# Routing weights of layer 1's experts: four products and on-chip transfers in place of sixteen products

## The chip, the cores and the metric

The kernel runs on one core of a Trainium2 chip. The metric is the device time of one execution in microseconds (us); a lower time is better. Three runs of the kernel before took 902.49, 902.59 and 903.48 us, so the median is 902.59 us.

## The reference, cut to what matters

The program is an eight-layer stack over x of shape (8, 256, 128), that is 2,048 tokens of 128 features, with a context of (8, 64, 128). Attention and feed-forward layers alternate. The change touches one of them, the mixture of experts of layer 1:

```
logits = x @ gate_w.T;  scores = sigmoid(logits)            # 64 experts
... the best 4 of 8 groups, then the best 8 experts of a token
topk_w = topk_w / (sum(topk_w) + 1e-20) * 2.5
rw = zeros((T, 64)).at[token, topk_idx].add(topk_w)         # (2048, 64) routing weights
expert_out[e] = (silu(x @ Wg[e].T) * (x @ Wu[e].T)) @ Wd[e].T    # hidden width 88
routed = einsum('eth,te->th', expert_out, rw)
shared = (silu(x @ Sg.T) * (x @ Su.T)) @ Sd.T               # hidden width 176
x = x + routed + shared
```

Every expert is computed for every token; the routing weight scales the expert's hidden values before the product with Wd.

## The kernel before, in words

Tokens lie on the free axis, as four groups q of 512 columns; weights, hidden units and features lie on the 128 partitions. The 64 experts' 88 hidden units are dealt into 44 chunks of 128 rows, so that 11 chunks in a row belong to the same 16 experts' share, eight rows for each expert: row p of a chunk has a routing weight of expert 16 e + p // 8, where e is the chunk's number modulo 4. A unit n is one chunk with one token group: 176 units, written out for the first 16 (`chunk_group1(0, True)` on TensorE, s = 0 to 15), then in a loop of 16 units a turn.

For each unit TensorE makes a gate product into bank s % 2 and an up product into bank 2 + s % 2 (`gate_up1`), three matmuls each, since an fp32 operand is split in a high and a low half of type fp32r and the two halves of both sides are multiplied in three of four pairs. ScalarE applies Silu to the gate (`silu1`). VectorE multiplies up by silu and then by the routing row (`hidden1`, lines 1852 and 1857; `hid_done`). ScalarE rounds the result to its high half (`hidden1_high`, line 925; `hh_hi`), GpSimd subtracts to get the low half (`hidden1_low`, line 734; `hh_lo`), and TensorE makes the down product of unit n three units behind (`down1`), into banks 4 to 7, which gather over all chunks. Weights come by DMA from SyncE's queue, and are halved by ScalarE (`gate_up1_high`, `down1_high`) and GpSimd (`gate_up1_low`, `down1_low`), one chunk ahead.

Nothing orders the work but the order in which each engine's program is written and its semaphore waits. Each engine runs its instructions in order.

Before the down products can start, the routing weights have to be spread. `rwb` is a tile of 128 partitions by 4 quarters e by 2,048 tokens: rwb[p, e, t] is the weight of expert 16 e + p // 8 for token t. The kernel before makes it so, in `routing_rows` and its counterparts:
- VectorE ends the routing with four multiplications (line 1834, `rw_done`); GpSimd copies each result beside itself (line 746, `rw_twice`), so that a transposed row is there twice.
- TensorE transposes 16 blocks (line 2501) into banks 4 to 7, after the copy of all four shared-expert results out of those banks (`sd_sb`). ScalarE copies each bank, rounded, into `rwr` (`rwr_hi`), and VectorE subtracts, for the lower 64 rows, the rounded value from the exact one (line 1842, `rwr_lo`): rows 0 to 63 of rwr are the high halves, rows 64 to 127 the low ones.
- TensorE multiplies `selr`, a 0/1 matrix that picks and repeats rows, with rwr: 16 products of 128x512 (names hh and selr), one for each quarter e and group q. Each goes to bank 4 + q; ScalarE copies even banks and VectorE odd ones (line 1845) to rwb, and TensorE waits for the copy of a bank before it writes the bank again.
- VectorE starts `hidden1(0)` after all copies. TensorE starts the third unit's gate product after all copies.

The gate and up products of units 0 and 1 stand ahead of this in TensorE's program, followed by the down products of the shared expert (`shared_down`, sdT). `uS` is a tile in the arena's tail that holds the shared expert's hidden values, eight blocks m. They are made in the stretch that precedes: TensorE's products (88x512), ScalarE's Silu and copy, GpSimd's multiplication (line 742).

SyncE's queue issues the loads of chunks 2 and 3 (`load_pair(0)`), then the convolution weights of layer 3 (in_conv), then the loads of the loop. A load waits until the halves of the chunk whose buffer it overwrites have been made. In the trace's names, arena and tail are one large scratch area each, psum is all banks, egu and edn are the loaded weights, xw holds token halves and gate/up weight halves, wdn the down weight halves.

Of the kernel before, what the change touches and what calls it, by code (L numbers as in the profile page):

```python
# [12 lines left out]
P = 128  # L13
# [13 lines left out]
RG = 4  # L27
# [19 lines left out]
def build_program(nc, A, out):  # L47
    with ExitStack() as ctx:
# [66 lines left out]
        selr = sb("selr", [P, RG, P], F32R)  # L115
# [114 lines left out]
        rw = carve(NT, 2, E1)  # L230
        rwr = hh[:, 2:4].rearrange("p k h n -> p (k h n)")
# [5 lines left out]
        sel1 = carve(RG, P)  # L237

# [79 lines left out]
        rwr_hi = sem("rwr_hi")  # L318
        rwr_lo = sem("rwr_lo")
# [82 lines left out]
        rw_twice = sem("rw_twice")  # L402
# [144 lines left out]
        def _(sp):  # L547
# [63 lines left out]
            load_pair(0)  # L611
# [18 lines left out]
        def _(pool):  # L630
# [105 lines left out]
            def experts1_low():  # L736
# [6 lines left out]
                for q in range(NG):  # L743
                    r = slice(4 * q, 4 * q + 4)
                    pool.wait_ge(rw_done, q + 1)
                    pool.tensor_copy(rw[:, r, 1, :], rw[:, r, 0, :]).then_inc(rw_twice, 1)
# [5 lines left out]
                def chunk_group(j, last=False):  # L752
                    for s in range(4 * RG):
                        ahead = s // 4 + 1
                        weights = not (last and ahead == RG)
                        if s % 4 == 1 and weights:
                            gate_up1_low(j * RG + ahead, ahead % 2)
# [41 lines left out]
            for L in range(LAYERS):  # L799
# [76 lines left out]
                if L == 2:  # L876
# [4 lines left out]
                    then(pool.affine_select(out=per_expert, in_=per_expert, compare_op=ALU.not_equal, fill=1.0, base=0,  # L881
                                            pattern=[[-1, E1], [0, 8]], channel_multiplier=1))
                    pool.affine_select(out=per_expert, in_=per_expert, compare_op=ALU.not_equal, fill=1.0, base=-E1,
# [39 lines left out]
        def _(act):  # L923
# [279 lines left out]
            act.wait_ge(pool_made, 2)  # L1203
            copy(selr[:, :, :], sel1)
            for m in range(2 * NG):
                act.wait_ge(sg_ready, m + 1)
                act.activation(silS[0:I1, m, :], psum[0:I1, 3 + m % 2, :], ACT.Silu)
                copy(uS[0:I1, m, :], psum[0:I1, 5 + m % 2, :]).then_inc(sil_s, 1)
            silu1(0, 0)
# [4 lines left out]
            for q in range(NG):  # L1214
                act.wait_ge(rw_tp, q + 1)
                copy(rwr[:, 512 * q:512 * q + 512], bank(4 + q)).then_inc(rwr_hi, 1)
            for k in range(2 * RG):
                act.wait_ge(rb_mm, 2 * k + 1)
                copy(rwb[:, k // 2, 1024 * (k % 2):1024 * (k % 2) + 512], bank(4 + 2 * (k % 2))).then_inc(rb_sb[0], 1)

            def chunk_group1(j, last=False):

                for s in range(4 * RG):
# [4 lines left out]
                    if later(j, 1) or s:  # L1228
                        hidden1_high(j * (4 * RG) + (s - 1), s - 1)
                    if s % 4 == 0 and weights:  # L1230
# [99 lines left out]
            def row2(k):  # L1330
                act.wait_ge(rb_mm, NG * RG + k + 1)
# [120 lines left out]
        def _(dve):  # L1452
# [335 lines left out]
            def routing():  # L1788
# [43 lines left out]
                for q in range(NG):  # L1832
                    r = slice(4 * q, 4 * q + 4)
                    dve.tensor_tensor(rw[:, r, 0, :], t3[:, r, :], wide(rsum1[:, 1, r].unsqueeze(2), 4, E1), ALU.mult).then_inc(rw_done, 1)
# [4 lines left out]
            for q in range(NG):  # L1839
                r = slice(512 * q, 512 * q + 512)  # L1840
                dve.wait_ge(rwr_hi, q + 1)
                dve.tensor_tensor(rwr[E1:P, r], psum[E1:P, 4 + q, :], rwr[E1:P, r].bitcast(F32), ALU.subtract).then_inc(rwr_lo, 1)
            for k in range(2 * RG):
                dve.wait_ge(rb_mm, 2 * k + 2)
                dve.tensor_copy(rwb[:, k // 2, 1024 * (k % 2) + 512:1024 * (k % 2) + 1024], bank(5 + 2 * (k % 2))).then_inc(rb_sb[1], 1)  # L1845
            dve.wait_ge(rb_sb[0], 2 * RG)
# [12 lines left out]
            for s in range(4 * RG):  # L1859
                hidden1(s, s)  # L1860
# [69 lines left out]
            dve.wait_ge(rb_mm, NG * RG + 1)  # L1930
            dve.tensor_copy(cB[:, 0, 0:512], bank(4)).then_inc(rb_sb[1], 1)

            def weighted2(n):
                dve.wait_ge(up_ready, DONE1 + n + 1)
                if n == 0:
                    dve.wait_ge(rb_sb[1], 2 * RG + 1)
                elif n < NG:
                    dve.wait_ge(rb_sb[0], 2 * RG + n)
                elif n == 4 * NG:
                    dve.wait_ge(rb_sb[0], 2 * RG + 2 * NG - 1)  # L1940
# [100 lines left out]
        def _(pe):  # L2041
# [453 lines left out]
            def routing_rows():  # L2495

                pe.wait_ge(sd_sb, NG)
# [409 lines left out]
```

## Time and profile before

| | |
|---|---|
| median of 3 runs | 902.59 us (902.49 to 903.48) |
| profiled execution | 902.16 us, span on the core 900.4 us |
| mean granted TensorE clock | 0.995 of full speed |
| busy over the span | PE 96%, PEld 74%, DVE 76%, ACT 60%, POOL 66% |
| DMA | 24.47 MB, mean 27 GB/s |
| layer 1's shared expert, gate and up | about 317 to 332 us of the span |
| shared down products | 332.15 to 339.46 us |
| routing rows | 340.15 to 349.4 us |
| 176 expert units | first units before 332 us, the rest from 349.4 us |

The span is the part of the execution in which the engines worked; 1.76 us of the profiled execution lie around it. A timeline row gives start, length, engine, line, operation, written and read names, and shape; xN is a count of instructions that stand together, and the length is from the start of the first to the end of the last. The bracket is idle time of the engine just before and what ended it. An fp32 matmul shows as two records, an fp32r one as one. The length of a single matmul includes its way through the array; matmuls of a row overlap, so the time one costs is read from the distance between starts.

### The profile page before, as it was taken

The numbers are of one execution on the slowest core, as the hardware profiler recorded it, in microseconds if no ns is written. First come the engines' busy times: TensorE is split into PE (matmuls) and PEld (weight loads), VectorE is DVE, ScalarE is ACT, GpSimd is POOL, SyncE is SP. The second block draws the span as 40 slices with busy tenths as digits, with TensorE's granted clock in tenths as the row PEclk, the third lists the DMA queues.
The fourth block names the chain that finished last, engine by engine and source line by source line (L and its number), as shares of the span: only waits on it lengthen the run. The fifth ranks groups of instructions, "written<-read, shape, count | busy, mean of one in ns | idle before, by whom it ended". The sixth has DMA issues, their size and how long they took to land.

```text
span 900.4 us, 16162 instructions
## 1 busy us (share of the span) xinstructions
PE 863.1 (96%) x4789; PEld 668.6 (74%) x4789; DVE 685.0 (76%) x1552; ACT 540.2 (60%) x1042; POOL 597.6 (66%) x622
## 2 busy tenths in 40 slices
PE   7998999999999998999999999999999998998997
PEld 5656676666697876888888888888888776775775
DVE  6998776899556798766666666666668778888886
ACT  3555667666753466666666666666666674445465
POOL 5983544688703346777777777777777777888720
PEclk9999999999999999999999999999999999999999
DMA  7000000322001001100000000000002000000001
GB/s 207 2 2 1 0 1 12 92 72 70 24 1 31 10 1 47 36 25 26 26 20 23 26 26 20 26 24 26 21 26 102 1 2 0 1 1 1 1 12 36
DMA packets 27433, 24.47 MB, mean 27 GB/s; under 512 B 3483, under 2 KB 24179, under 8 KB 27251
## 3 DMA queue, kind: packets, MB, share of 16 engines
q1 hardware_dynamic: 27379, 23.80, 8.9%
q8 instruction: 28, 0.46, 0.2%
q14 instruction: 26, 0.21, 0.1%
HBM read 22.74 MB, written 1.05 MB: 26 GB/s over the span
## 4 chain that ended last, share of the span: by engine, by line
PE 73%; DVE 13%; ACT 6%; POOL 5%; issue 2%; DVEq 0%; ACTq 0%; POOLq 0%
PE psum L2043 67%; POOL hh L771 3%; DVE arena L1952 2%; ACT hh L925 2%; PE psum L2208 2%; DVE arena L1594 2%; DVE arena L1591 1%; DVE stats L1468 1%; ACT arena L987 1%; PE psum L2285 1%; PE psum L2070 1%; PE psum L2101 1%; ACT arena L925 1%; ACT xn L1178 1%; DVE arena L1600 1%
## 5 line engine op out<-in xcount | busy, mean ns | idle before, releaser
L2043 PE MATMUL psum<-xw 128*128 128x512 f32 x1248 | 322.8, 394 | 1.7 <-DVE arena L1845 1.0
L734 POOL TENSOR_TENSOR hh<-arena,hh 128x512 fp32r<-128x512 f32 x176 | 228.1, 1296 | 81.7 <-ACT hh L925 80.3
L2043 PEld LDWEIGHTS psum<-xw 128*128 128x128 f32 x1248 | 232.3, 188 | 54.2 <-issue 3.8
L1852 DVE TENSOR_TENSOR psum<-psum,arena 128x512 f32<-128x512 f32 x176 | 123.1, 699 | 97.7 <-PE psum L2043 91.5
L1195 ACT ACTIVATE arena<-psum 128x512 f32<-128x512 f32 x176 | 105.4, 599 | 119.9 <-PE psum L2043 119.9
L925 ACT ACTIVATE hh<-arena 128x512 fp32r<-128x512 f32 x228 | 142.3, 625 | 38.2 <-DVE arena L1952 34.9
L2043 PE MATMUL psum<-hh,wdn 128*128 128x512 f32 x528 | 148.4, 390 | 0.2 <-POOL hh L734 0.2
L1857 DVE TENSOR_TENSOR arena<-psum,arena 128x512 f32<-128x512 f32 x176 | 121.7, 691 | 7.6 <-DVE psum L1852 1.7
L2043 PEld LDWEIGHTS psum<-hh,wdn 128*128 128x128 f32 x528 | 98.9, 188 | 21.1 <-POOL hh L734 0.5
L2043 PE MATMUL psum<-arena 128*32 128x128 f32 (+6 forms) x992 | 85.6, 303 | 3.8 <-ACT arena L925 2.4
L925 ACT ACTIVATE arena<-psum 128x512 f32<-128x512 f32 (+6 forms) x85 | 57.4, 687 | 44.3 <-PE psum L2043 19.8
L2043 PEld LDWEIGHTS psum<-arena 128*32 128x32 f32 (+3 forms) x992 | 59.5, 142 | 16.7 <-issue 8.4
L771 POOL TENSOR_TENSOR hh<-arena,hh 128x512 fp32r<-128x512 f32 x48 | 61.3, 1295 | 9.1 <-ACT hh L925 9.1
L869 POOL TENSOR_TENSOR tail<-tail 128x512 f32<-128x512 f32 x32 | 33.3, 1039 | 36.5 <-DVE tail L1617 36.5
L705 POOL TENSOR_TENSOR arena<-arena,xn (+1 forms) x32 | 46.3, 1451 | 1.2 <-ACT xn L925 1.2
L682 POOL TENSOR_TENSOR rstd<-veps,neghalf 128x4 f32<-128x4 f32 (+1 forms) x19 | 18.3, 965 | 43.1 <-DVE veps L1480 33.3
L1006 ACT ACTIVATE tail<-arena,tail 128x256 f32<-128x256 f32 x64 | 32.0, 500 | 24.6 <-DVE tail L1581 24.6
L2043 PE MATMUL psum<-hh,w2r 128*128 128x512 f32 x144 | 43.8, 410 | 0.8 <-POOL hh L771 0.8
L2043 PE MATMUL psum<-xw,w2r 128*128 128x512 f32 x144 | 42.0, 402 | 0.9 <-DVE arena L1952 0.5
L1057 ACT ACTIVATE tail<-psum,ebias 128x512 f32<-128x512 f32 x32 | 22.0, 688 | 30.3 <-PE psum L2043 29.8
L694 POOL TENSOR_TENSOR xw<-egu,xw 128x256 fp32r<-128x256 f32 x32 | 25.4, 796 | 22.2 <-ACT xw L925 22.2
L1952 DVE SCALAR_TENSOR_TENSOR arena<-psum,arena 128x512 f32<-128x512 f32 x48 | 33.2, 691 | 7.7 <-POOL hh L771 7.5
(310 smaller groups left out, 1501.4 us busy)
## 6 DMA issues: line engine op xcount, KB each, us to landing
egu<-in_w SPq DMA_DIRECT2D x44, 128.0 KB, 2.0
egu<-in_egu SPq DMA_DIRECT2D x16, 256.0 KB, 2.6
edn<-in_w SPq DMA_DIRECT2D x44, 64.0 KB, 1.8
edn<-in_edn SPq DMA_DIRECT2D x16, 128.0 KB, 2.1
arena<-in_w SPq DMA_DIRECT2D x1, 1536.0 KB, 7.1
X<-in_x SPq DMA_DIRECT2D x4, 256.0 KB, 5.0
arena<-in_ctxTd SPq DMA_DIRECT2D x2, 512.0 KB, 6.0
arena<-in_conv SPq DMA_DIRECT2D x1, 768.0 KB, 4.2
```

The source lines that it names most:

```text
L694: pool.tensor_tensor(wgu_pair(f, 1), egu_part(k, f), wgu_pair(f, 0).bitcast(F32), ALU.subtract).then_inc(wgu_lo, 1)
L705: pool.tensor_tensor(part, part, wide(shift_row(b).unsqueeze(1), 2, N), ALU.subtract).then_inc(pt_shifted, 1)
L734: pool.tensor_tensor(hh[:, s % 4, 1, :], h1[:, s % 2, :], hh[:, s % 4, 0, :].bitcast(F32), ALU.subtract).then_inc(hh_lo, 1)
L771: pool.tensor_tensor(hh[:, n % 4, 1, :], h2[:, n % 2, :], hh[:, n % 4, 0, :].bitcast(F32), ALU.subtract).then_inc(hh_lo, 1)
L869: pool.tensor_tensor(qb[:, k % 4], qb[:, k % 4], wide(recB[:, k % 4].unsqueeze(2), 2, N), ALU.mult)\
L925: return act.activation(dst, src, ACT.Copy)
L1006: last = act.activation(qb[:, k % 4, c, :], logit_part(k // 4, 2 * (k % 4) + c, 1).rearrange("p a n -> p (a n)"), ACT.Exp, scale=-1.0, bia ...
L1195: act.activation(sil[:, k, :], bank(k), ACT.Silu).then_inc(nl_done, 1)
L1852: dve.tensor_tensor(bank(2 + k), bank(2 + k), sil[:, k, :], ALU.mult).then_inc(prod_done, 1)
L1857: dve.tensor_tensor(h1[:, k, :], bank(2 + k), rwb[:, s // 4, own], ALU.mult).then_inc(hid_done, 1)
L1952: dve.scalar_tensor_tensor(h2[:, n % 2, :], bank(n % NG), 0.0, v2w[:, n % 3, :], ALU.max, ALU.mult).then_inc(hid_done, 1)
L2043: return pe.matmul(dst, lhsT=lhsT, rhs=rhs, start=start, stop=stop)
```

## The change

The four multiplications that end the routing write `rw` without a gap, and GpSimd's four copies, the split in halves, `selr` and its copy, and `rwr` are gone. TensorE transposes blocks of 64 rows, each bank as soon as the shared result in it has been copied. ScalarE copies the four banks, 64 partitions each, as plain fp32 to `rwf`, which takes the place of the first half of uS (`rwf_sb`). TensorE then makes four fp32 products with the first quarter of sel1: these give rwb's quarter e = 0; VectorE copies the first bank and ScalarE the other three. Quarters 1 to 3 are written by 24 DMAs from SyncE's queue, each from 16 neighbouring partitions of rwf (2,048 floats, 8 KB each) to every eighth partition of rwb; they wait for all four copies. VectorE waits for the first eight at unit 4 (`rwb_second`) and for the other sixteen at unit 8 (`rwb_rest`). The loads of chunk 3, and so the convolution's, stand behind the 24 in the queue.

The gate/up halves of chunk 1 move ahead, to the place behind block m = 5 of the shared expert on ScalarE and on GpSimd. ScalarE's `hidden1_high(0)` moves in between its copies of rwb. TensorE's third unit no longer waits for the rows; the first four down products wait for the copy of their bank instead.

The diff, cut to its core (left out are renamed semaphores and shifted counts in layer 2's waits):

```
-        selr = sb("selr", [P, RG, P], F32R)
...
-        rw = carve(NT, 2, E1)
-        rwr = hh[:, 2:4].rearrange("p k h n -> p (k h n)")
+        rw = carve(2, NT, E1)[:, 0]
...
         uS = carve(2 * NG, 512)
         sel1 = carve(RG, P)
+        rwf = uS[:, 0:NG, :].rearrange("p q n -> p (q n)")
...
-            load_pair(0)
+            load_gu(2, 0, 1)
+            load_dn(2, 0, 1)
+            sp.wait_ge(rwf_sb, NG)
+            for e in range(1, RG):
+                for i in range(8):
+                    sp.dma_start(rwb[i:P:8, e, :], rwf[16 * e:16 * e + 16, :]).then_inc(rwb_in[e > 1], 16)
+            load_gu(3, 1, 2)
+            load_dn(3, 1, 2)
...
                     pool.tensor_tensor(uS[0:I1, m, :], uS[0:I1, m, :], silS[0:I1, m, :], ALU.mult).then_inc(hs_done, 1)
-                for q in range(NG):
-                    r = slice(4 * q, 4 * q + 4)
-                    pool.wait_ge(rw_done, q + 1)
-                    pool.tensor_copy(rw[:, r, 1, :], rw[:, r, 0, :]).then_inc(rw_twice, 1)
+                    if m == 5:
+                        gate_up1_low(1, 1)
                 for g in range(NG):
                     pool.wait_ge(sd_sb, g + 1)
...
-                        if s % 4 == 1 and weights:
+                        if s % 4 == 1 and weights and (later(j, 1) or s > 1):
                             gate_up1_low(j * RG + ahead, ahead % 2)
...
-                    then(pool.affine_select(out=per_expert, in_=per_expert, compare_op=ALU.not_equal, fill=1.0, base=0,
-                                            pattern=[[-1, E1], [0, 8]], channel_multiplier=1))
-                    pool.affine_select(out=per_expert, in_=per_expert, compare_op=ALU.not_equal, fill=1.0, base=-E1,
+                    pool.affine_select(out=per_expert, in_=per_expert, compare_op=ALU.not_equal, fill=1.0, base=0,
                                        pattern=[[-1, E1], [0, 8]], channel_multiplier=1).then_inc(pool_made, 1)
...
-            act.wait_ge(pool_made, 2)
-            copy(selr[:, :, :], sel1)
             for m in range(2 * NG):
                 act.wait_ge(sg_ready, m + 1)
                 act.activation(silS[0:I1, m, :], psum[0:I1, 3 + m % 2, :], ACT.Silu)
                 copy(uS[0:I1, m, :], psum[0:I1, 5 + m % 2, :]).then_inc(sil_s, 1)
+                if m == 5:
+                    gate_up1_high(1, 1, 8 * E0 + 16)
...
             for q in range(NG):
                 act.wait_ge(rw_tp, q + 1)
-                copy(rwr[:, 512 * q:512 * q + 512], bank(4 + q)).then_inc(rwr_hi, 1)
-            for k in range(2 * RG):
-                act.wait_ge(rb_mm, 2 * k + 1)
-                copy(rwb[:, k // 2, 1024 * (k % 2):1024 * (k % 2) + 512], bank(4 + 2 * (k % 2))).then_inc(rb_sb[0], 1)
+                copy(rwf[0:E1, 512 * q:512 * q + 512], psum[0:E1, 4 + q, :]).then_inc(rwf_sb, 1)
+            for q in range(1, NG):
+                act.wait_ge(rb_mm, q + 1)
+                copy(rwb[:, 0, 512 * q:512 * q + 512], bank(4 + q)).then_inc(rb_sb[0], 1)
+                if q == 1:
+                    hidden1_high(0, 0)
...
-                    if later(j, 1) or s:
+                    if later(j, 1) or s > 1:
                         hidden1_high(j * (4 * RG) + (s - 1), s - 1)
-                    if s % 4 == 0 and weights:
+                    if s % 4 == 0 and weights and (later(j, 1) or s):
...
-                    dve.tensor_tensor(rw[:, r, 0, :], t3[:, r, :], wide(rsum1[:, 1, r].unsqueeze(2), 4, E1), ALU.mult).then_inc(rw_done, 1)
+                    dve.tensor_tensor(rw[:, r, :], t3[:, r, :], wide(rsum1[:, 1, r].unsqueeze(2), 4, E1), ALU.mult).then_inc(rw_done, 1)
...
-            for q in range(NG):
-                r = slice(512 * q, 512 * q + 512)
-                dve.wait_ge(rwr_hi, q + 1)
-                dve.tensor_tensor(rwr[E1:P, r], psum[E1:P, 4 + q, :], rwr[E1:P, r].bitcast(F32), ALU.subtract).then_inc(rwr_lo, 1)
-            for k in range(2 * RG):
-                dve.wait_ge(rb_mm, 2 * k + 2)
-                dve.tensor_copy(rwb[:, k // 2, 1024 * (k % 2) + 512:1024 * (k % 2) + 1024], bank(5 + 2 * (k % 2))).then_inc(rb_sb[1], 1)
-            dve.wait_ge(rb_sb[0], 2 * RG)
+            dve.wait_ge(rb_mm, 1)
+            dve.tensor_copy(rwb[:, 0, 0:512], bank(4)).then_inc(rb_sb[1], 1)
+            dve.wait_ge(rb_sb[1], 1)
...
             for s in range(4 * RG):
+                if 1 <= s < NG:
+                    dve.wait_ge(rb_sb[0], s)
+                if s == NG:
+                    dve.wait_ge(rwb_in[0], 16 * 8)
+                if s == 2 * NG:
+                    dve.wait_ge(rwb_in[1], 16 * 8 * (RG - 2))
                 hidden1(s, s)
...
-                pe.wait_ge(sd_sb, NG)
                 for q in range(NG):
-                    pe.wait_ge(rw_twice, q + 1)
+                    pe.wait_ge(sd_sb, SD_BANKS.index(4 + q) + 1)
+                    pe.wait_ge(rw_done, q + 1)
                     for j in range(4):
-                        last = pe.transpose(psum[:, 4 + q, P * j:P * j + P], rw[:, 4 * q + j].rearrange("p k e -> p (k e)"), ident[:, :])
+                        last = pe.transpose(psum[0:E1, 4 + q, P * j:P * j + P], rw[:, 4 * q + j, :], ident[:, :])
                     last.then_inc(rw_tp, 1)
...
-                for k in range(NG * RG):
-                    e, q = k // NG, k % NG
-                    if e >= 1:
-                        pe.wait_ge(rb_sb[q % 2], 2 * e + q // 2 - 1)
-                    else:
-                        pe.wait_ge(rwr_lo, q + 1)
-                    mm(bank(4 + q), selr[:, e, :], rwr[:, 512 * q:512 * q + 512]).then_inc(rb_mm, 1)
+                pe.wait_ge(pool_made, 2)
                 for q in range(NG):
-                    pe.wait_ge(rb_sb[q % 2], 2 * RG + q // 2 - 1)
+                    pe.wait_ge(rwf_sb, q + 1)
+                    mm(bank(4 + q), sel1[0:E1, 0, :], rwf[0:E1, 512 * q:512 * q + 512]).then_inc(rb_mm, 1)
...
+                    if first and s < 3 + NG:
+                        pe.wait_ge(rb_sb[s == 3], 1 if s == 3 else s - 3)
                     down1(j * (4 * RG) + (s - 3), s - 3, slot if s % 4 == 3 else 1 - slot, first and s < 7, last and s == 4 * RG - 1)
```

How this moves the instructions is seen in the order of each engine's program. TensorE, from the end of the shared down products to the first down product of an expert (MATMUL rows of 128x128 on ident are transposes; hh,selr are the rows' products, xw gate and up, hh,wdn down), before:

```order
L2043 MATMUL psum<-sdT,tail 128x128 x32
L2501 MATMUL psum<-ident,arena 128x128 x16
L2043 MATMUL psum<-hh,selr 128x512 x16
L2043 MATMUL psum<-xw 128x512 x12
L2043 MATMUL psum<-hh,wdn 128x512 x3
```

and now (psum<-tail are the four fp32 products):

```order
L2047 MATMUL psum<-sdT,tail 128x128 x32
L2505 MATMUL psum<-ident,arena 64x128 x16
L2047 MATMUL psum<-tail 128x512 x4
L2047 MATMUL psum<-xw 128x512 x12
L2047 MATMUL psum<-hh,wdn 128x512 x3
```

Twelve products less stand between the transposes and the units.

VectorE from the end of the routing to unit 4, with the semaphores waited for, before:

```order
L1842 TENSOR_TENSOR hh<-psum,hh 64x512 [waits rwr_hi] x4
L1845 COPY arena<-psum 128x512 [waits rb_mm] x8
L1852 TENSOR_TENSOR psum<-psum,arena 128x512 [waits nl_done,up_ready,rb_sb_act]
L1857 TENSOR_TENSOR arena<-psum,arena 128x512 [waits prod_done]
L1852 TENSOR_TENSOR psum<-psum,arena 128x512 [waits nl_done,up_ready]
```

and now, with the rows of unit 4 and of unit 8 below the "...":

```order
L1843 COPY arena<-psum 128x512 [waits rb_mm]
L1850 TENSOR_TENSOR psum<-psum,arena 128x512 [waits nl_done,up_ready,rb_sb_dve]
L1855 TENSOR_TENSOR arena<-psum,arena 128x512 [waits prod_done]
L1850 TENSOR_TENSOR psum<-psum,arena 128x512 [waits nl_done,up_ready,rb_sb_act]
...
L1850 TENSOR_TENSOR psum<-psum,arena 128x512 [waits nl_done,up_ready,rwb_second]
...
L1850 TENSOR_TENSOR psum<-psum,arena 128x512 [waits nl_done,up_ready,rwb_rest]
```

Eleven instructions are gone, and two new waits stand ahead of units 4 and 8.

SyncE's queue from the loads of chunk 2 on, now (before, the two rows on tail are not there):

```order
L594 DMA egu<-in_w 128x256 [waits wgu_lo]
L598 DMA edn<-in_w 128x128 [waits wdn_lo]
L614 DMA arena<-tail 16x2048 [waits rwf_sb]
L614 DMA arena<-tail 16x2048 x23
L594 DMA egu<-in_w 128x256 [waits wgu_lo]
L598 DMA edn<-in_w 128x128 [waits wdn_lo]
L618 DMA arena<-in_conv 128x1536 [waits hid_done]
```

The 24 transfers stand between the loads of chunk 2 and those of chunk 3.

## Rows read from the trace of the kernel before

**Rows 1.** The page: busy time of each engine, and the chain that ended last.

```profile
PE 863.1 (96%) x4789; PEld 668.6 (74%) x4789; DVE 685.0 (76%) x1552; ACT 540.2 (60%) x1042; POOL 597.6 (66%) x622
PE 73%; DVE 13%; ACT 6%; POOL 5%; issue 2%; DVEq 0%; ACTq 0%; POOLq 0%
```

**Rows 2.** The chain of waits in order of time, 339 to 351 us: start, length, what.

```profile
339.50 0.61 ACT arena L925
...
344.02 2.58 DVE arena L1845 x4
...
350.69 34.36 PE psum L2043 x150
```

**Rows 3.** Timeline of TensorE, 332 to 356 us.

```profile
332.15 7.31 PE L2043 MATMUL psum<-sdT,tail 88*128 88x128 f32 x64
...
340.15 1.97 PE L2501 MATMUL psum<-ident,arena 128*128 128x128 f32 x16 [0.69 <-ACT arena L925]
...
352.87 0.88 PE L2043 MATMUL psum<-hh,wdn 128*128 128x512 f32 x3
...
355.65 1.52 PE L2043 MATMUL psum<-xw 128*128 128x512 f32 x6
357.01 0.84 PE L2043 MATMUL psum<-hh,wdn 128*128 128x512 f32 x3
...
365.85 1.52 PE L2043 MATMUL psum<-xw 128*128 128x512 f32 x6
```

**Rows 4.** Timeline of TensorE near 314 us: one fp32 product, and what follows.

```profile
314.01 1.02 PE L2043 MATMUL psum<-xnT,sgT 128*88 128x512 f32 x2
314.87 0.60 PE L2070 MATMUL psum<-ident,xn 128*128 128x128 f32 x4
```

**Rows 5.** Timeline of the other engines, 325 to 351 us.

```profile
329.00 6.25 POOL L742 TENSOR_TENSOR tail<-tail,arena 88x512 f32<-88x512 f32 x5 [1.23 <-DVE arena L1818]
...
329.63 0.59 ACT L1207 ACTIVATE arena<-psum 88x512 f32<-88x512 f32 x1 [0.32 <-PE psum L2043]
...
340.84 2.07 ACT L925 ACTIVATE hh<-psum 128x512 fp32r<-128x512 f32 x4 [0.75 <-PE psum L2501]
...
348.62 0.41 ACT L925 ACTIVATE xw<-egu 128x256 fp32r<-128x256 f32 x1
349.10 0.73 POOL L726 TENSOR_TENSOR xw<-egu,xw 128x256 fp32r<-128x256 f32 x1 [3.60 <-ACT xw L925]
349.21 0.70 DVE L1852 TENSOR_TENSOR psum<-psum,arena 128x512 f32<-128x512 f32 x1
...
349.94 0.69 DVE L1857 TENSOR_TENSOR arena<-psum,arena 128x512 f32<-128x512 f32 x1
350.67 0.63 ACT L925 ACTIVATE hh<-arena 128x512 fp32r<-128x512 f32 x1 [1.65 <-DVE arena L1857]
```

**Rows 6.** Timeline: unit 8 on VectorE; GpSimd's low half; two DMA issues of SyncE's queue.

```profile
363.35 0.70 DVE L1852 TENSOR_TENSOR psum<-psum,arena 128x512 f32<-128x512 f32 x1 [0.61 <-PE psum L2043]
...
363.85 1.29 POOL L734 TENSOR_TENSOR hh<-arena,hh 128x512 fp32r<-128x512 f32 x1 [0.32 <-ACT hh L925]
...
356.37 0.43 SPq L613 DMA_DIRECT2D arena<-in_conv  x1
356.84 0.43 SPq L614 DMA_DIRECT2D arena<-in_conv  x1
```

**Rows 7.** DMA issues: count, KB each, median us from issue to landing.

```profile
arena<-in_w SPq DMA_DIRECT2D x1, 1536.0 KB, 7.1
...
out<-X SPq DMA_DIRECT2D x3, 256.0 KB, 2.3
...
out<-X SPq DMA_DIRECT2D x2, 64.0 KB, 1.7
```

**Rows 8.** Busy time of each engine by stretch; PEclk is the granted clock.

```profile
745.00:750.00 5.00, 3.33 (x26) 1.80 (x26) 3.28 (x9) 2.11 (x4) 3.35 (x1) 1.00 0.00 0
750.00:755.00 5.00, 4.36 (x12) 2.49 (x12) 4.63 (x9) 3.93 (x8) 2.65 (x4) 0.70 0.00 0
```

More of the change, by code:

```diff
@@ L317, in build_program @@
         hh_lo = sem("hh_lo")
-        rwr_hi = sem("rwr_hi")
-        rwr_lo = sem("rwr_lo")
+        rwf_sb = sem("rwf_sb")
+        rwb_in = [sem("rwb_second"), sem("rwb_rest")]
         x_done = sem("x_done")
@@ L401, in build_program @@
         sd_sb = sem("sd_sb")
-        rw_twice = sem("rw_twice")
         rb_mm = sem("rb_mm")
@@ L1330, in row2 @@
             def row2(k):
-                act.wait_ge(rb_mm, NG * RG + k + 1)
+                act.wait_ge(rb_mm, NG + k + 1)
                 copy(cB[:, k // NG, 512 * (k % NG):512 * (k % NG) + 512], bank(4 + k % NG)).then_inc(rb_sb[0], 1)
@@ L1929, in _ @@
             dve.tensor_copy(cT[0:3 * E2, 0:1024], bank(4).bitcast(BF16)[0:3 * E2, :]).then_inc(rw_sb[0], 1)
-            dve.wait_ge(rb_mm, NG * RG + 1)
+            dve.wait_ge(rb_mm, NG + 1)
             dve.tensor_copy(cB[:, 0, 0:512], bank(4)).then_inc(rb_sb[1], 1)
@@ L1935, in weighted2 @@
                 if n == 0:
-                    dve.wait_ge(rb_sb[1], 2 * RG + 1)
+                    dve.wait_ge(rb_sb[1], 2)
                 elif n < NG:
-                    dve.wait_ge(rb_sb[0], 2 * RG + n)
+                    dve.wait_ge(rb_sb[0], NG - 1 + n)
                 elif n == 4 * NG:
-                    dve.wait_ge(rb_sb[0], 2 * RG + 2 * NG - 1)
+                    dve.wait_ge(rb_sb[0], 3 * NG - 2)
                 if n >= 3:
@@ L2671, in down2 @@
                 if n < NG:
-                    pe.wait_ge(rb_sb[0], 2 * RG + NG + n)
+                    pe.wait_ge(rb_sb[0], 2 * NG - 1 + n)
                 pe.wait_ge(hh_hi, DONE1 + n + 1)
@@ L2692, in combine_rows2 @@
                     if e:
-                        pe.wait_ge(rb_sb[q == 0], 2 * RG + max(q, 1))
+                        pe.wait_ge(rb_sb[q == 0], 2 if q == 0 else NG - 1 + q)
                     mm(bank(4 + q), sel2[0:3 * E2, e, :], cT[0:3 * E2, 512 * q:512 * q + 512]).then_inc(rb_mm, 1)
```

## The prediction

> **What bounds the kernel now.** I read the page first, then the chain of waits, then the timeline around the change. On the page TensorE is busy 96% of the span and is 73% of the chain [rows 1], so time is won only where it idles or does work that can go. The reader is to see in the chain that it leaves TensorE between 339.5 and 350.7 us: ScalarE's last shared copy, the transposes, VectorE's copies of the rows, the first hidden values [rows 2]. From 350.69 us on it is TensorE again for 34 us. In TensorE's timeline the shared down products end at 332.15 + 7.31 = 339.46 us, and the first expert's down product begins at 352.87 us [rows 3]: 13.4 us, of which all that is not needed later is the stake. From there on a unit costs (365.85 - 355.65) / 5 = 2.04 us, nine matmuls of 0.227 us back to back [rows 3]; the other engines only have to keep up.
>
> **What goes and what comes on TensorE.** Between 339.46 us and the first down product the new program has:
> - 16 transposes, 1.97 us as now [rows 3]. The 0.69 us of waiting ahead of them goes: the first bank's shared result was copied earlier, and the last copy (339.50 to 340.11 us, [rows 2]) is wanted only by the third group of transposes, at 340.4 us.
> - Four fp32 products. One of that kind was followed by the next instruction 314.87 - 314.01 = 0.86 us later [rows 4]; 4 x 0.86 = 3.44 us. The sixteen that go were cheap ones that waited for copies.
> - The 12 matmuls of units 2 and 3: six take 357.01 - 355.65 = 1.36 us [rows 3], so 2.72 us.
>
> The sum is 8.13 us, the first down product begins at 347.6 us, and that is 5.3 us earlier than 352.87.
>
> **Whether something else is late there.** ScalarE's copies to rwf follow the transposes at 0.5 us each (four take 2.07 us, [rows 5]), with the first bank done at about 340.1 us and the last copy at 342.3 us; TensorE comes to the first product at 341.4 us. That product ends at 342.3 us, VectorE copies it (0.65 us) and makes hidden(0) in 0.70 + 0.69 us [rows 5], done at 344.5 us; the up product of unit 2, which needs it, is due at 345.6 us. The first down product needs hidden(0)'s two halves, 0.63 us [rows 5] and 1.29 us [rows 6] behind it: 346.5 us against 347.6 us. ScalarE's two remaining copies stand between, 0.5 us each, and put Silu of unit 2 at 346.1 to 346.7 us and the halves of unit 1 at 348.6 us, against 349.7 us for the second down product. Each cover is about 1 us, so I charge nothing; if all were gone, 1 us of the 5.3 would be.
>
> **The halves of chunk 1** add 0.41 us of ScalarE and 0.73 us of GpSimd [rows 5] to the shared stretch. ScalarE idled 0.32 us before a Silu there, and the blocks 6 and 7 behind the insertion are wanted late. GpSimd's multiplications ended at 335.25 us [rows 5]; at 336.0 us they are still ahead of the last shared down product at about 337.7 us, a quarter of 7.31 before 339.46. Nothing is charged. At the other end the two halves leave the place where VectorE's copies hid them.
>
> **The 24 transfers.** SyncE is released at 342.3 us, first issue 342.4 us. Two issues in a row stand 0.47 us apart [rows 6], so 24 take 11.3 us, the last issued at 353.7 us. What they cost depends on the rate, which no row shows for an SBUF source of 16 partitions. The nearest rows are stores of X, which read all 128 partitions: 64 KB land in 1.7 us and 256 KB in 2.3 us [rows 7], so 196,608 bytes in 0.6 us are 328 GB/s, and 1.5 us are fixed. The load of 1,536 KB in 7.1 us [rows 7] gives (7.1 - 1.5) the same order, 281 GB/s. The 24 move 3.146 MB.
> - Upper end: the partitions read don't matter. At 328 GB/s the bytes take 9.6 us, less than the issues, and all have landed by 355.6 us.
> - Lower end: the rate goes with the partitions read, an eighth, 41 GB/s. The bytes take 77 us, and all have landed at 421 us.
>
> The deadline follows from the units. Unit 8 begins on VectorE at 363.35 us now [rows 6], 358.1 us then; TensorE runs dry if hidden(8) (1.45 us) ends behind its up product of unit 10, now at 365.85 + 0.68 = 366.5 us, then 361.3 us. So the sixteen are due at 359.8 us, for which 197 GB/s suffice, and the first eight, four units of 2.04 us earlier, at 351.6 us, for which 1.049 MB need 136 GB/s. At 149 GB/s the wait eats exactly the 5.3 us.
>
> Neither end has a near row: the stores read everything, and here sixteen readers meet on an eighth of the partitions. I take the middle in ratio, the root of 41 x 328 = 116 GB/s. Then the bytes take 27.1 us, the first eight have landed at 342.4 + 9.0 + 1.5 = 352.9 us, and TensorE idles 1.3 us; all have landed at 371.0 us, hidden(8) ends at 372.5 us, and the up product of unit 10 begins then instead of at 366.5 us: 6.0 us later than before. The idle stretch is about 10 us. An idle stretch also costs clock: behind a stretch in which TensorE was busy 3.33 of 5 us it ran the next 5 us at 0.70 of the clock [rows 8], so partly at the lower level (1.2 GHz of 2.4), and 5 x 0.30 = 1.5 us were lost. I add 1.7 us for this longer stretch. The loads of chunk 3 land right behind, within 1 us, while TensorE is catching up.
>
> The page "SBUF — State Buffer" of the Trainium skill (section "Door 1: The DMA port swizzle") speaks against this change: the rate goes with the SBUF ports that the partitions reach, sixteen neighbours reach four of sixteen, and partitions 0..15 measured 104 GB/s. [...] An estimate by that page would be 30.2 us for the bytes, all landed at 374.1 us, and 913.4 us in all; my own sum does without it.
>
> **The sum.** +6.0 + 1.7 = +7.7 us on the profiled execution of 902.16 us, which lies 0.43 us under the median of 902.59 us: 910.3 us against the median.
>
> **The rivals.**
> - Full rate (32%). The on-chip transfers run like the stores, are bound by their issues and land at 355.6 us, 4.2 us ahead of the deadline; the first eight land at 342.4 + 3.8 + 1.9 = 348.1 us, 3.5 us ahead. Chunk 3's loads, issued at 353.7 us, are there by 356 us for ScalarE, which wants them at about 358.4 us. Then nothing is late and the gain stands: 902.6 - 5.3 = 897.3 us. For it: each of the sixteen rows can have an engine of its own, the runs are 8 KB long, and the load shows that large runs flow well. Against: nothing shows that 16 partitions can be read at 197 GB/s.
> - Break-even (9%). A rate of 140 to 165 GB/s, so the rows arrive about where the old ones did, and the wait at unit 8 takes what was won: 901 to 905 us.
> - Rate near the lower end (4%). At 60 to 80 GB/s the bytes take 39 to 52 us: 922 to 936 us. Same mechanism as my forecast, further out.
>
> **How the numbers follow.** My forecast, slower by the wait at unit 8, has 55%, with a range of its own from 905 to 915 us (about 140 down to 100 GB/s). With the rivals: faster by over 0.2% (1.8 us, about what a measurement of this kernel can tell from no change) 34%, the full rate and a little of the next; within it 7%; slower 59%, the forecast, the far rival and what is left of break-even. The range must reach to the full rate, since that has more than 2 in 10: 896.8 to 915 us.
>
> **What would show it.** Right or wrong in the profile after: the first expert's down product at 347.6 us; no wait on VectorE before unit 0 to 3 beyond TensorE's; VectorE idle before unit 4 by some 3 us (352.9 us against 363.35 - 4 x 2.04 - 5.3 = 349.9 us) and before unit 8 by some 10 us, released by a DMA; DMA moving at 110 to 120 GB/s from 343 to 370 us; a granted clock under 1.00 behind it. If the 24 transfers land within 14 us of the first issue and VectorE shows no wait for them, the step of the rate is wrong and 897 us is the time. If the first down product is not near 347.6 us, the sum on TensorE is wrong, whatever the transfers do.

## The result, and the profile after

The changed kernel takes 919.18 us (median of 4 runs, 917.46 to 920.95), the kernel before 903.04 us beside it: ratio 1.018, 95% interval 1.0167 to 1.0193, slower by 16.1 us. The profiled execution took 919.24 us, its span is 917.4 us and the mean granted clock 0.978. Forecast were 910.3 us and a range of 896.8 to 915: the direction holds, the size is more than twice the forecast's.

The page of the kernel after, busy time and the chain that ended last; these answer to [rows 1]:

```profile
PE 872.1 (95%) x4781; PEld 673.7 (73%) x4781; DVE 679.8 (74%) x1541; ACT 537.3 (59%) x1036; POOL 595.6 (65%) x617
PE 69%; DVE 13%; ACT 6%; POOL 5%; SPq 3%; issue 2%; DMA 1%; DVEq 0%; ACTq 0%; POOLq 0%
```

TensorE has 9.0 us more of busy time for eight instructions fewer. The last experiment, e9, has the same 4781 instructions and 859.7 us of busy time; the 12.4 us between those two are not work but a lower clock. The chain now holds 3% of SyncE's queue and 1% of DMA, together 4% of 917 us, which TensorE's 73% have given up.

TensorE's timeline after, 337 to 386 us (start, length, engine, line, what, and in brackets the idle time before and what ended it); these answer to [rows 3]:

```profile
337.83 1.84 PE L2047 MATMUL psum<-sdT,tail 88*128 88x128 f32 x15
342.84 2.58 PE L2505 MATMUL psum<-ident,arena 128*64 128x128 f32 x16 [3.17 <-DVE arena L1837]
345.35 7.19 PE L2047 MATMUL psum<-tail 64*128 64x512 f32 x8
...
357.67 0.85 PE L2047 MATMUL psum<-hh,wdn 128*128 128x512 f32 x3
...
370.62 0.84 PE L2047 MATMUL psum<-xw 128*128 128x512 f32 x3
379.28 1.65 PE L2047 MATMUL psum<-xw 128*128 128x512 f32 x3 [7.82 <-DVE arena L1855]
...
385.41 1.55 PE L2047 MATMUL psum<-xw 128*128 128x512 f32 x6
```

TensorE has two holes. In the first one, 3.17 us, it waits for VectorE's routing rows, and what stands behind it runs at half speed: the four fp32 products take 7.19 us. The first down product begins at 357.67 us, where 347.6 was forecast and 352.87 was the time before. The second hole is the forecast's: 7.82 us ahead of the up product of unit 10.

The first hole's cause stands in the timelines of VectorE and GpSimd after, 334 to 343 us:

```profile
334.89 2.72 DVE L1831 SCALAR_TENSOR_TENSOR arena<-arena 128x1024 f32<-128x1024 f32 x1
...
338.90 1.11 DVE L1833 TENSOR_SCALAR arena<-arena 128x16 f32<-128x16 f32 x1
...
340.33 3.37 DVE L1837 TENSOR_TENSOR arena<-arena 128x256 f32<-128x256 f32 x4
336.49 5.92 POOL L753 TENSOR_TENSOR X<-X,arena 128x512 f32<-128x512 f32 x4
```

The same in the kernel before, 334 to 346 us:

```profile
334.28 2.04 DVE L1828 SCALAR_TENSOR_TENSOR arena<-arena 128x1024 f32<-128x1024 f32 x1
...
337.61 0.17 DVE L1830 TENSOR_SCALAR arena<-arena 128x16 f32<-128x16 f32 x1
...
338.11 1.83 DVE L1834 TENSOR_TENSOR arena<-arena 128x256 f32<-128x256 f32 x4
340.51 4.99 POOL L750 TENSOR_TENSOR X<-X,arena 128x512 f32<-128x512 f32 x4
```

GpSimd's four additions of the shared result to X stood behind its four copies of `rw`, which waited for VectorE. The change deletes the copies, and with them the only thing that held the additions back: they now begin 4.0 us earlier, beside the end of VectorE's routing. There the large step that reads two SBUF operands took 2.72 us instead of 2.04, the tiny one 1.11 instead of 0.17, and the four multiplications 3.37 instead of 1.83. The first of the four took 2.37 us and ended at 342.7 us, just behind GpSimd's last addition (342.41 us); the other three took 0.41 us each. e1 below shows that the additions are the cause.

The second hole's cause shows in SyncE's queue and on VectorE at unit 8, kernel after:

```profile
346.07 27.70 SPq L614 DMA_DIRECT2D arena<-tail  x24
377.80 0.70 DVE L1850 TENSOR_TENSOR psum<-psum,arena 128x512 f32<-128x512 f32 x1 [10.30 <-DMA arena<-tail]
```

24 transfers of 131,072 bytes are 3.146 MB. From the first issue to the release of unit 8 are 31.7 us; less the 1.5 us that the prediction takes as fixed, 30.2 us: 104 GB/s. The issues fill 27.7 us, 1.15 us each on average, where the forecast took the 0.47 us of [rows 6]. Most of that is the transfers' own pace, which held SyncE's queue up, but not all: the shortest of these issues takes 0.585 us (see e8).

The clock by stretch, kernel after (start and end, length, busy time of TensorE, its weight loads, VectorE, ScalarE and GpSimd with instruction counts, granted TensorE clock, DMA share, GB/s):

```profile
344.00:350.00 6.00, 6.00 (x13) 2.86 (x12) 2.29 (x4) 2.57 (x6) 0.00 (x0) 0.50 0.54 57
350.00:356.00 6.00, 6.00 (x11) 3.24 (x11) 1.34 (x3) 2.78 (x6) 1.93 (x2) 0.50 0.94 96
356.00:358.00 2.00, 2.00 (x7) 1.59 (x6) 1.30 (x3) 1.22 (x2) 0.62 (x1) 0.61 1.00 156
358.00:370.00 12.00, 12.00 (x55) 9.91 (x54) 8.08 (x12) 6.20 (x12) 9.47 (x9) 1.00 0.95 108
370.00:378.00 8.00, 1.46 (x7) 0.88 (x5) 0.20 (x1) 0.00 (x0) 0.00 (x0) 0.79 0.91 122
378.00:384.00 6.00, 4.72 (x11) 3.80 (x12) 5.21 (x8) 3.43 (x7) 3.28 (x3) 0.50 0.68 209
...
860.00:865.00 5.00, 4.60 (x22) 3.83 (x23) 4.75 (x20) 0.94 (x3) 2.62 (x4) 0.77 0.00 0
```

Behind each hole the chip granted 0.50, that is 1.2 GHz: for 13 us after the first one, though TensorE was busy all the while, and for 6 us after the second. From 386 us on the kernel after runs 15.5 us behind the kernel before, and that stays so until 860 us. There its granted clock fell once more, to 0.77 over 5 us, where the kernel before kept 1.00, and it ends 17.0 us behind. e3 and e8 show this late dip too, e1, e2, e4 and e9 don't; what brings it on stays open, and no experiment here explains it.

### The profile page after: what moved, and what is told of

Same layout as the page of the kernel before. It is cut to its first block, busy times and chain, and to the rows that moved or that the text cites. A ratio compares the mean times of both kernels' runs of the same rounds, so it can differ in the third digit from the quotient of the medians.

```text
span 917.4 us, 16152 instructions
## 1 busy us (share of the span) xinstructions
PE 872.1 (95%) x4781; PEld 673.7 (73%) x4781; DVE 679.8 (74%) x1541; ACT 537.3 (59%) x1036; POOL 595.6 (65%) x617
## 4 chain that ended last, share of the span: by engine, by line
PE 69%; DVE 13%; ACT 6%; POOL 5%; SPq 3%; issue 2%; DMA 1%; DVEq 0%; ACTq 0%; POOLq 0%
PE psum L2047 63%; POOL hh L774 3%; SPq L614 3%; DVE arena L1956 2%; ACT hh L926 2%; PE psum L2212 1%; DVE arena L1597 1%; DVE arena L1594 1%; DVE stats L1471 1%; PE psum L2105 1%; ACT arena L988 1%; PE psum L2289 1%; PE psum L2074 1%; DMA wv<-in_wv 1%; DMA arena<-tail 1%
## 5 line engine op out<-in xcount | busy, mean ns | idle before, releaser
L2047 PE MATMUL psum<-xw 128*128 128x512 f32 x1248 | 327.1, 398 | 8.2 <-DVE arena L1855 7.8
L2047 PEld LDWEIGHTS psum<-xw 128*128 128x128 f32 x1248 | 235.0, 190 | 63.1 <-DVE arena L1855 8.2
L926 ACT ACTIVATE arena<-psum 128x512 f32<-128x512 f32 (+7 forms) x80 | 54.4, 693 | 47.3 <-PE psum L2047 22.6
L699 POOL TENSOR_TENSOR xw<-egu,xw 128x256 fp32r<-128x256 f32 x32 | 25.9, 809 | 21.8 <-ACT xw L926 21.8
L731 POOL TENSOR_TENSOR xw<-egu,xw 128x256 fp32r<-128x256 f32 x44 | 33.6, 765 | 8.8 <-ACT xw L926 8.8
```

The lines of the kernel that those rows point to most:

```text
L731: pool.tensor_tensor(wgu[:, slot, 1, :], w1gu(slot), wgu[:, slot, 0, :].bitcast(F32), ALU.subtract).then_inc(wgu_lo, 1)
L926: return act.activation(dst, src, ACT.Copy)
L2047: return pe.matmul(dst, lhsT=lhsT, rhs=rhs, start=start, stop=stop)
```

## The experiments

Nine kernels ran, e1 to e4 beside runs of the kernel before with a median of 903.27 us, e5 to e8 beside 902.72, e9 beside 902.61. The code below shows of each experiment the lines that matter; the rest is left out. Two causes were suspected: the early additions (with the clock behind them), and the transfers' rate. e1 undoes the first, e2 the second, e3 both; e4 takes the transfers away.

**e1: the additions held back.** On GpSimd, after the blocks of the shared expert:

```
+                pool.wait_ge(rw_done, NG)
                 for g in range(NG):
                     pool.wait_ge(sd_sb, g + 1)
```

> The changed kernel, but GpSimd's four additions to X wait until VectorE has made all four blocks of rw. Theory (GpSimd's additions and VectorE's last routing steps, which both read two SBUF operands, hold each other up): VectorE's steps at lines 1831 to 1837 are back to 2.04, 0.17 and 0.42 us, the transposes start within 0.3 us of the end of the shared down products instead of 3.2 us behind it, TensorE's clock stays at 1.00 until 360 us, and the first expert's down product starts at 347.8 us instead of 357.7. The transfers start 3.6 us earlier and still take 31.7 us, so the wait at unit 8 stays: 915.6 us. Rival (the lateness comes from something else, such as chunk 1's halves on GpSimd): VectorE's steps stay long and the time stays at 919 us.

Measured: 913.17 us, ratio 1.011 (1.0088 to 1.0132); 6.0 us less than the kernel after. Timelines of VectorE, GpSimd and TensorE of e1:

```profile
338.36 1.43 DVE L1838 TENSOR_TENSOR arena<-arena 128x256 f32<-128x256 f32 x4
339.87 4.94 POOL L754 TENSOR_TENSOR X<-X,arena 128x512 f32<-128x512 f32 x4 [2.17 <-DVE arena L1838]
...
339.64 1.92 PE L2506 MATMUL psum<-ident,arena 128*64 128x128 f32 x16
341.49 3.70 PE L2048 MATMUL psum<-tail 64*128 64x512 f32 x8
345.12 3.06 PE L2048 MATMUL psum<-xw 128*128 128x512 f32 x12
348.01 0.84 PE L2048 MATMUL psum<-hh,wdn 128*128 128x512 f32 x3
...
357.72 0.98 PE L2048 MATMUL psum<-xw 128*128 128x512 f32 x3 [4.11 <-DVE arena L1856]
375.12 1.65 PE L2048 MATMUL psum<-xw 128*128 128x512 f32 x3 [7.32 <-DVE arena L1856]
```

With the additions behind the rows the multiplications take 1.43 us, TensorE has no hole, and the first down product begins at 348.01 us: 9.7 us earlier than in the kernel after, and 0.4 us from the forecast. What is left is the transfers: 27.16 us of issues, hardly less than before, a hole of 4.11 us for the first eight (which land at 356.24 us) and one of 7.32 us at the up product of unit 10, now at 375.12 us against 379.28. So only 4.2 us of the 9.7 arrive there; the rest had been standing in the shadow of the slow transfers.

**e2: the sources spread over 64 partitions.** VectorE writes the experts in another order, so that the sixteen rows of a quarter lie on every fourth partition of rwf; GpSimd's selection pattern follows.

```
-  sp.dma_start(rwb[i:P:8, e, :], rwf[16 * e:16 * e + 16, :])
+  sp.dma_start(rwb[i:P:8, e, :], rwf[e:E1:RG, :])
```

> The changed kernel, but the 64 experts' rows are laid in rwf so that a quarter's sixteen rows stand on every fourth partition (0, 4, ... 60 for the first) instead of on sixteen neighbours; the 24 transfers, their sizes and destinations stay. Theory (the rate depends on which SBUF partitions are read): the rate about doubles, from 104 to about 208 GB/s, all have landed 16.6 us after the first issue instead of 31.7, VectorE has no wait at unit 8, and what is left of the loss is TensorE's lateness at the first down product (357.7 against 352.9 us, 4.8 us): 907.9 us. Rival (sixteen runs of 8 KB a transfer, or the write side, set the rate): nothing moves, 919 us.

Measured: 907.21 us, ratio 1.0035 (1.0017 to 1.0053), 12.0 us less than the kernel after. The queue of e2:

```profile
347.54 15.71 SPq L614 DMA_DIRECT2D arena<-tail  x24
```

15.71 us for the issues instead of 27.70, and VectorE waits at neither unit 4 nor unit 8. The first hole (3.27 us) and the low clock behind it are as in the kernel after. Bytes, number and length of the transfers are unchanged; of the transfers only where the sixteen rows lie is different. (VectorE's multiplications write in a strided order for it, about 0.58 us each instead of 0.41.)

**e3: both.**

> Both of the former edits together. If both theories hold: transfers start at 342.5 us and have landed by 359.1 us, just ahead of 359.8 us when TensorE would run dry, the first expert's down product starts at 347.8 us, the clock stays up, and the time is 898 us, 5 us under the kernel before. If only the additions matter: 915.6 us. If only the partitions matter: 908 us.

Measured: 899.5 us, ratio 0.9955 (0.9938 to 0.9972): faster than the kernel before by 3.8 us in the medians. The first down product is at 348.00 us, and the granted clock 1.00 from 339 to 390 us. One wait is left:

```profile
342.37 16.66 SPq L614 DMA_DIRECT2D arena<-tail  x24
361.00 0.70 DVE L1852 TENSOR_TENSOR psum<-psum,arena 128x512 f32<-128x512 f32 x1 [3.19 <-DMA arena<-tail]
362.48 0.97 PE L2049 MATMUL psum<-xw 128*128 128x512 f32 x3 [0.72 <-DVE arena L1857]
```

361.00 - 342.37 - 1.5 = 17.1 us for 3.146 MB: 184 GB/s. This is no longer a limit of the source: e8 below shows that the issues set this pace.

**e4: no transfers at all.** The 24 DMAs and VectorE's two waits are left out, three quarters of the expanded rows are unwritten; the additions stay early.

> The changed kernel without the 24 transfers and without VectorE's two waits for them, so three quarters of the routing rows are not written. It tells what the rest of the change costs. If all of the loss beyond the late start of the units is the transfers' wait and its clock: first down product at 357.7 us as in the changed kernel, no wait at units 4 and 8, 907.9 us. If the transfers cost more than their wait (traffic, issue time in SyncE's queue): below 907 us.

Measured: 906.91 us, ratio 1.0035 (1.0013 to 1.0056), the same as e2: once the rows are spread, the transfers cost nothing beside the first hole. What is left above the kernel before is the first hole's doing.

**e6: e4 with the hole filled.** To split the hole from the clock, twelve matmuls whose result is not used stand ahead of the transposes on TensorE:

```
             def routing_rows():
+                pe.wait_ge(nl_done, 2)
+                busy(0, 12)
```

> The kernel of e4 (no transfers, GpSimd's additions still early) with twelve fp32 128 x 128 matmuls into a free bank on TensorE, ahead of the routing transposes, where TensorE waited 3.2 us for VectorE's rows. Their result is not used. Three quarters of the rows are unwritten, as in e4. Theory (the idle stretch sent the clock to 1.2 GHz, and that is most of what e4 costs over the forecast): clock 1.00 from 340 to 360 us, transposes, products and unit matmuls at 1.92, 3.70 and 3.06 us instead of 3.60, 7.19 and 5.40, the first down product at about 351.3 us instead of 358.5, and 906.9 - 7.2 = 899.7 us. Rival (the transposes and the products of 64 partitions lower the clock themselves): clock 0.50 all the same, 906.9 us.

Measured: 901.38 us, ratio 0.9983 (0.9974 to 0.9993). TensorE of e4, then of e6:

```profile
342.61 3.60 PE L2497 MATMUL psum<-ident,arena 128*64 128x128 f32 x16 [3.20 <-DVE arena L1833]
346.13 7.19 PE L2039 MATMUL psum<-tail 64*128 64x512 f32 x8
...
358.49 0.85 PE L2039 MATMUL psum<-hh,wdn 128*128 128x512 f32 x3
```

```profile
338.40 2.84 PE L2039 MATMUL psum<-ident 128*128 128x128 f32 x24
341.75 1.91 PE L2499 MATMUL psum<-ident,arena 128*64 128x128 f32 x16 [0.51 <-DVE arena L1833]
343.59 3.70 PE L2039 MATMUL psum<-tail 64*128 64x512 f32 x8
...
350.07 0.84 PE L2039 MATMUL psum<-hh,wdn 128*128 128x512 f32 x3
```

The rows came no earlier, measured from the shared products' end, but the clock stayed at 1.00: from the transposes to the first down product are 8.3 us instead of 15.9. So the transposes and the 64-partition products don't lower the clock; the hole ahead of them does, and 7.6 us of the 358.49 - 350.07 = 8.4 us are its price. In the medians it is less, 4.7 us (1.0035 - 0.9983, times 903): e4's runs reach from 902.41 to 911.02 us and e6's from 899.83 to 904.51. The clocks of single runs of e4 (0.980 to 0.991) suggest that it doesn't fall for as long in each of them; no trace of those runs shows it.

**e7: the chunk 1 halves alone**, in the kernel before. The edit is the change's own two lines at m = 5 on ScalarE and on GpSimd, and the conditions that leave them out later.

> The kernel before with nothing but the halves of chunk 1 moved behind block m = 5 of the shared expert, on ScalarE and GpSimd. Theory (they are hidden at both places, as forecast): 903.0 us, the same. Rival (they hold up GpSimd's products or ScalarE's Silu in the shared stretch, or free VectorE's way in the first units): up to 1.1 us to either side, 901.9 or 904.1 us.

Measured: 903.31 us, ratio 1.0009 (1.0000 to 1.0018), and the first down product at 352.48 us in its trace (352.87 before). Moving them neither costs nor gives anything that counts.

**e8: every second partition of 32**, in e3. The rows are then those of other experts.

```
-  rwf[e:E1:RG, :]
+  rwf[32 * (e % 2):32 * (e % 2) + 32:2, :]
```

> The kernel of e3, but each of the 24 transfers reads every second partition of a block of 32 instead of every fourth of 64 (the data are then those of other experts). Theory (what counts is how many ports the sixteen partitions reach: by the table in the page SBUF - State Buffer of the Trainium skill every second of 32 reaches eight, as does every fourth of 64, and sixteen neighbours four): the 24 issues take 16.7 us as in e3, 899.5 us. Rival (what counts is how far the sixteen partitions lie apart, so the rate is half way between that of neighbours and of every fourth, about 140 GB/s): bytes 22.5 us, all landed at 366.4 us, TensorE idle about 6 us and the time about 905 us.

Measured: 898.8 us, ratio 0.9953 (0.9938 to 0.9969). A stretch of 5 us within the transfers, of the kernel after, then of e3, then of e8 (the last two numbers are the DMA share and GB/s):

```profile
350.00:355.00 5.00, 5.00 (x9) 2.49 (x9) 1.18 (x2) 2.32 (x5) 1.26 (x1) 0.50 0.89 90
```

```profile
345.00:350.00 5.00, 5.00 (x22) 4.05 (x22) 3.62 (x6) 4.19 (x9) 3.49 (x4) 1.00 0.56 198
```

```profile
345.00:350.00 5.00, 5.00 (x23) 4.09 (x23) 3.53 (x6) 4.16 (x9) 3.56 (x3) 1.00 0.95 207
```

By the same count as above e8 runs at 188 GB/s (360.02 - 341.76 - 1.5 = 16.8 us), e3 at 184. Both numbers are the pace of SyncE's issues. The 24 issues and their landings in the kernel after, then in e3, then in e8 (shortest, middle and longest issue in ns; shortest, middle and longest time from issue to landing in us):

```profile
L614 SPq DMA_DIRECT2D arena<-tail x24: 585/1243/2617, 346.1 to 372.5; - x24
DMA to landing us min/median/max: 3.3/5.3/5.6
```

```profile
L614 SPq DMA_DIRECT2D arena<-tail x24: 486/592/1416, 342.4 to 358.4; - x24
DMA to landing us min/median/max: 2.5/2.6/3.7
```

```profile
L614 SPq DMA_DIRECT2D arena<-tail x24: 493/591/791, 341.8 to 356.9; - x24
DMA to landing us min/median/max: 2.4/2.7/3.1
```

An issue takes 0.59 us in e3 and in e8 alike, and the shortest ones of the kernel after take the same. In e3 and e8 the typical transfer lands 2.6 or 2.7 us behind its issue, so hardly any backlog builds up; in the kernel after it takes 5.3 us. So 184 and 188 GB/s are lower bounds for the two spread sources, and what either could give with faster issues isn't measured. What e8 does rule out is the rival that counts distance, which wanted 140 GB/s: half the distance between the rows is enough.

By the table of "SBUF — State Buffer" of the Trainium skill (section "Door 1: The DMA port swizzle") sixteen neighbours reach four ports, every second of 32 and every fourth of 64 both reach eight. The runs agree with it in that the neighbours alone are held to 104 GB/s; that eight ports give twice the rate of four no run here shows, since the issues come first. The two spread sources also differ in something: the busy share of the DMA engines, the number ahead of the GB/s, is 0.56 in e3 and 0.95 in e8 for about the same bytes, and 0.89 in the kernel after for half of them. So it doesn't tell the rate; why it differs stays open.

**e5: a wait for each quarter**, in e3: unit 8 waits for the third quarter, unit 12 for the fourth.

```
-                if s == 2 * NG:
-                    dve.wait_ge(rwb_in[1], 16 * 8 * (RG - 2))
+                if s == 2 * NG:
+                    dve.wait_ge(rwb_in[1], 16 * 8)
+                if s == 3 * NG:
+                    dve.wait_ge(hc_sb, 1 + 16 * 8)
```

> The kernel of e3 with one wait per quarter: VectorE waits at unit 8 for the third quarter alone and at unit 12 for the fourth. In e3 the wait at unit 8 ended at 361.0 us, 3.19 us late on VectorE, and left TensorE idle for 0.72 us. Theory (the fourth quarter is not needed before unit 12, and the third has landed when two thirds of the bytes have, at about 342.4 + 11.4 + 1.5 = 355.3 us): no wait at 8 or 12, TensorE's 0.72 us are won, 898.8 us against 899.5. Rival (transfers land mixed, the third quarter hardly ahead of the fourth): 899.5 us, the same wait.

Measured: 898.0 us, ratio 0.9948 (0.9934 to 0.9962). VectorE no longer waits for a DMA, but ScalarE, then VectorE and TensorE behind it, do:

```profile
360.85 0.42 ACT L927 ACTIVATE xw<-egu 128x256 fp32r<-128x256 f32 x1 [2.74 <-DMA egu<-in_w]
363.33 0.97 PE L2051 MATMUL psum<-xw 128*128 128x512 f32 x3 [0.26 <-DVE arena L1857]
```

The loads of chunk 3 stand behind the 24 in SyncE's queue and were issued at 358.5 us.

**e9: those loads ahead of the fourth quarter**, in e5.

```
             for e in range(1, RG):
+                if e == 3:
+                    load_gu(3, 1, 2)
+                    load_dn(3, 1, 2)
```

> The kernel of e5 with the two loads of chunk 3 issued between the transfers of the third and of the fourth quarter instead of behind all 24. In e5 ScalarE waited 2.74 us for the gate/up load, until 360.85 us, and TensorE then idled 0.26 us at the up product of unit 10. Theory (that load is the last thing late there): issued at about 353 us it lands by about 358 us, ScalarE's wait falls under 0.5 us, TensorE shows no wait between the first down product and 370 us, and the time is 897.7 us, 0.3 under e5 and not to be told from it. Rival (the fourth quarter, now about 1 us and the load's bytes later, becomes late for unit 12, or the load crawls among the transfers): a wait of VectorE for a DMA at unit 12, and 898 to 899 us.

Measured: 897.52 us, ratio 0.9945 (0.9922 to 0.9968). TensorE and the stretch of e9:

```profile
346.79 0.84 PE L2052 MATMUL psum<-hh,wdn 128*128 128x512 f32 x3
...
371.27 0.84 PE L2052 MATMUL psum<-hh,wdn 128*128 128x512 f32 x3
```

```profile
340.00:370.00 30.00, 30.00 (x127) 23.12 (x125) 24.03 (x35) 19.79 (x39) 24.97 (x24) 1.00 0.50 165
```

The first down product and that of the twelfth unit behind it are 24.48 us apart, 12 x 2.04, so nothing waits there any more, at the full clock. The 0.5 us to e5 can't be told from no difference; both are faster than the kernel before by some 5 us.

## Why the prediction was wrong in size

**The sum on TensorE** (first down product at 347.6 us) was right for the instructions and wrong for this kernel, as the prediction's own sign says. Where the rows are on time, e1 and e3 begin at 348.0 us; in e1 the steps are 1.85, 3.63 and 2.89 us from start to start (339.64, 341.49, 345.12, 348.01) where the forecast had 1.97, 3.44 and 2.72. In the kernel after it was 357.67 us.

**The step that failed** is "Nothing is charged" for GpSimd. I followed what the change adds there (the halves, rightly nothing: e7) and what it removes (the copies), but not what the copies held back. The next thing in GpSimd's program, the additions, could run as soon as the shared results were there, and ran beside VectorE. The 0.69 us of waiting ahead of the transposes, which was to go, became 3.17 us, and that one sent the clock down, which cost more than the wait did (7.6 us in e4 against e6). My cover estimates of 1 us around the rows all began with rows that were on time. e1 undoes this step alone: the wait is gone, the first down product is at 348.01 us instead of 357.67, and the time 6.0 us less.

**The rate** was taken as 116 GB/s and measured as 104: first issue to unit 8 took 31.7 us instead of the 28.6 that 27.1 + 1.5 gave. That the mean in ratio of two ends a factor of 8 apart came within 12% is luck; it had no mechanism behind it. The estimate by "SBUF — State Buffer" of the Trainium skill (section "Door 1: The DMA port swizzle") in the prediction, 30.2 us for the bytes at its 104 GB/s, agrees with this trace (30.2 us, the same 1.5 us taken off). The page doesn't say whether it measured into SBUF or out of it; here the sixteen partitions are read. The landings inside the transfers were less even than assumed: in e1 the wait for the first eight ended 13.85 us behind the first issue, not 10.5, and made a hole of 4.11 us where 1.3 was forecast; the later hole would have come anyway.

**The clock behind the wait** was put at 1.7 us. The up product of unit 10 came 12.75 us later than before (379.28 against 366.53) and the first product of unit 12 15.5 us later (385.41 against 369.93): 2.7 us.

Together: forecast +7.7; SyncE's release at 346.07 instead of 342.4, +3.7; the transfers, +3.1; the clock behind, +1.0. That is +15.5 us, measured +16.1 in the medians and +17.1 in the profiled execution, of which 1.5 come at the late dip of the clock at 860 us. The 3.7 us reach the end whole because the transfers start with the rows; the 6.5 us that the slow clock took from TensorE between 343 and 358 us (14.8 us from the transposes to the first down product, 8.4 in e1) do not add to them, since TensorE had to wait for unit 8 in any case.

**The likeliest case** was the right one: the wait at unit 8, released by a DMA, 10 us on VectorE (10.30), about 110 GB/s in the windows. The wait of some 3 us at unit 4 did not show, because the units themselves came late; e1, with the rows on time, has it, 6.07 us long. The rival of the full rate, 897.3 us, has about the time that e3, e5 and e9 reach once rows and additions are put right (899.5, 898.0, 897.5). But it had one more number wrong: it took 0.47 us for an issue and let all transfers land at 355.6 us. An issue of these takes 0.59 us, and from one to the next 0.65 to 0.69 (15.71 and 16.66 us for 24), so in e3 unit 8 was released at 361.00 us, behind the 359.8 us that the prediction gives as the deadline. Even with a source that keeps up the change as written is a little late at unit 8; e5 and e9 get the rest by waiting for less and by loading earlier, and not by a faster transfer.

## What to carry to other kernels

When an instruction goes, look at what stood behind it in its engine's program: what it was waiting for has been delaying that too, and what runs early can land on an engine that is on the path. When a short wait appears on TensorE, price the clock behind it and not the wait. For on-chip copies don't let all transfers read the same sixteen neighbouring partitions: here another order of the experts, at 0.58 instead of 0.41 us for a VectorE multiplication, was worth 12 us. And price an issue by one of the same shape: 0.47 us was that of another transfer, 0.59 that of these.

## What the runs showed of the hardware

- Some VectorE steps from SBUF to SBUF stood still beside GpSimd's additions: 0.17 us became 1.11 and 0.41 us became 2.37, where one addition takes 1.27. The reduction (1.22 us) and the reciprocal (0.25 us) between them took as long as before. Steps with one operand in PSUM kept their 0.69 to 0.70 us beside the same additions (e1).
- TensorE idle for 3.2 us was followed by 13 us at 1.2 GHz though it was busy throughout; with 0.5 us of idle time there it stayed at 2.4 GHz (e6).
- The same 24 transfers ran at 104 GB/s from sixteen neighbouring partitions, and at 184 and 188 GB/s, the pace of their issues, from every fourth of 64 and every second of 32.
- An issue of these transfers takes 0.59 us on SyncE when nothing holds it up, and 1.24 us (the median of the 24) when the transfers can't keep up, so loads behind them in the queue are late as well (373.81 us here).
